# One scatter and one gather in turn, instead of four scatters and then four gathers

## The reference, cut to what matters

```python
row, col = edge_index[0], edge_index[1]                 # src, dst; the edges are sorted by dst
edge_input = concatenate([x[row], x[col], edge_attr])   # 128 + 128 + 16
h    = silu(edge_input @ eW1 + eb1)
m_ij = silu(h @ eW2 + eb2)
agg  = segment_sum(m_ij, row, num_segments=50000)
update = silu(concatenate([x, agg]) @ nW1 + nb1) @ nW2 + nb2
out  = layernorm(x + (x + update))
```

## Time and profile before

| | |
|---|---|
| median of the runs | 1695.71 us |
| the profiled execution, its own time | 1696.16 us |
| its span in the trace | 1694.7 us |
| granted TensorE clock over the span | 0.989 |
| PE busy | 1387.3 us, 82% |
| PE weight loads | 958.4 us, 57% |
| DVE busy | 939.6 us, 55% |
| ACT busy | 400.0 us, 24% |
| POOL busy | 1030.0 us, 61% |
| gathers L327, 392 | 384.3 us |
| scatters L370, 392 | 388.5 us |

### The profile page before, as it was taken

How to read it: one execution, slowest core, us unless ns; L and a number is a source line. 1 busy time by engine, 2 the same in 40 slices (tenths; PEclk the granted TensorE clock), 3 DMA queues, 4 the chain that set the end, 5 groups by cost and what they waited for, 6 DMA issues and landing times.

```text
span 1694.7 us, 25381 instructions
## 1 busy us (share of the span) xinstructions
PE 1387.3 (82%) x7834; PEld 958.4 (57%) x7834; DVE 939.6 (55%) x2971; ACT 400.0 (24%) x766; POOL 1030.0 (61%) x956
## 2 busy tenths in 40 slices
PE   1057888888888888888888888799997999999996
PEld 1054544444444444444444444455556999999996
DVE  6004555555555565555655556466763666666665
ACT  0001111111111111111111111121222555555555
POOL 7722666666666666666666666543444666666664
PEclk9999999999999999999999999899998999999998
DMA  9994343333433333333333333333326999999984
GB/s 376 412 365 115 89 112 101 105 105 100 112 100 106 106 100 110 102 106 106 100 110 102 103 108 100 89 97 102 96 94 222 305 297 301 305 299 302 304 297 161
DMA packets 156845, 284.99 MB, mean 168 GB/s; under 512 B 28046, under 2 KB 92322, under 8 KB 156708
## 3 DMA queue, kind: packets, MB, share of 16 engines
q1 hardware_dynamic: 110020, 162.78, 31.2%
q0 software_dynamic: 25088, 52.23, 10.8%
q10 hardware_dynamic: 21600, 68.32, 10.4%
HBM read 188.31 MB, written 94.91 MB: 167 GB/s over the span
## 4 chain that ended last, share of the span: by engine, by line
PE 60%; issue 14%; DVE 14%; another core or an unknown queue 11%; SPq 1%; DMA 0%; ACT 0%; POOL 0%; DVEq 0%; ACTq 0%
PE psum L544 10%; PE psum L534 8%; PE psum L489 7%; PE psum L486 7%; DVE junk L734 7%; PE psum L473 5%; PE psum L531 5%; PE psum L510 4%; PE psum L498 4%; DVE onehot L727 4%; PE psum L515 3%; PE psum L445 2%; DVE q L749 2%; PE psum L501 1%
## 5 line engine op out<-in xcount | busy, mean ns | idle before, releaser
L734 DVE CUSTOM_DVE_ANT_0 junk<-onehot,psum 128x625 f16<-128x625 f16 x392 | 316.4, 807 | 473.8 <-remote 232.9
L327 POOL DMA_INDIRECT x_src<-x_d,idx_src x392 | 384.3, 980 | 290.9 <-issue 129.4
L370 POOL DMA_INDIRECT table<-q,pos x392 | 388.5, 991 | 209.3 <-issue 113.7
L486 PE MATMUL psum<-onehot,after 128*128 128x512 f16 (+1 forms) x782 | 169.7, 298 | 178.8 <-issue 110.9
L486 PEld LDWEIGHTS psum<-onehot,after 128*128 128x128 f16 x782 | 51.8, 97 | 417.6 <-issue 416.8
L576 ACT ACTIVATE hT<-psum,b_e 128x512 f32<-128x512 f32 x98 | 67.4, 687 | 740.7 <-remote 617.0
L430 POOL TENSOR_TENSOR rstd<-var_eps,minus_half 128x5 f32<-128x5 f32 (+1 forms) x79 | 135.6, 1717 | 153.9 <-DVE var_eps L794 153.9
L473 PE MATMUL psum<-pick,window 128*128 128x128 f32 x1568 | 194.3, 278 | 7.2 <-DMA window<-x_d 7.2
L473 PEld LDWEIGHTS psum<-pick,window 128*128 128x128 f32 x1568 | 185.9, 195 | 7.6 <-DMA window<-x_d 7.6
L544 PE MATMUL psum<-w_out,uT 128*128 128x128 f32 (+1 forms) x782 | 188.5, 388 | 0.0
L544 PEld LDWEIGHTS psum<-w_out,uT 128*128 128x128 f32 (+1 forms) x782 | 178.9, 314 | 0.0
(11 more groups left out here) (85 smaller groups left out, 1533.5 us busy)
## 6 DMA issues: line engine op xcount, KB each, us to landing
window<-x_d SPq DMA_DIRECT2D x392, 128.0 KB
slots_in<-table SPq DMA_DIRECT2D x79, 528.0 KB, 5.0
table<-empty ACTq DMA_DIRECT2D x9, 4224.0 KB
x_in<-x_d SPq DMA_DIRECT2D x78, 320.0 KB, 4.2
xT_in<-xT_d SPq DMA_DIRECT2D x78, 320.0 KB, 3.8
out<-y_out ACTq DMA_DIRECT2D x78, 320.0 KB, 4.1
place<-place_dram SPq DMA_DIRECT2D x98, 128.0 KB
x_src<-x_d,idx_src POOLq DMA_INDIRECT x392
```

The costliest lines, as they stand in the source:

```text
L327: pool.indirect_dma_start(rows, None, x[:, :], bass.IndirectOffsetOnAxis(ap=idx[:, g * TILES + t:g * TILES + t + 1], axis=0)).then_inc(don ...
L370: pool.indirect_dma_start(table[:, :], bass.IndirectOffsetOnAxis(ap=pos[:, g * TILES + t:g * TILES + t + 1], axis=0), q[g % Q][:, t, :], None,
L486: nc.tensor.matmul(p_rank[:, cols], after[:], earlier[:, cols], start=False, stop=False, skip_group_check=True)
L734: V.tensor_tensor_reduce(out=junk[:], in0=onehot[g % 2][:, t, :], in1=p_rank, scale=1.0, scalar=0.0, op0=ALU.mult, op1=ALU.add, accum_out= ...
```

## The change

The function `scatter(g)` and the call of `gather_src(g + LEAD)` behind it become one function. It takes all waits first and then issues one scatter and one gather in turn, four times. Where there is no group left to gather (the last 22 of the 98 rounds) it only scatters.

```diff
-            def scatter(g):
+            def scatter_and_gather(g, ahead):
 
                 wait(pool, s_q, 2 * (g + 1))
                 wait(pool, s_pos, g + 1)
+                if ahead < GROUPS:
+                    wait(pool, s_src_turned, ahead - X_SRC + 1)
                 for t in range(TILES):
                     pool.indirect_dma_start(
                         table[:, :], bass.IndirectOffsetOnAxis(ap=pos[:, g * TILES + t:g * TILES + t + 1], axis=0),
                         q[g % Q][:, t, :], None,
                     ).then_inc(s_scattered[g % Q], 16)
+                    if ahead < GROUPS:
+                        gather(x_src[ahead % X_SRC][:, t * D:(t + 1) * D], idx_src, ahead, t, s_gathered[ahead % X_SRC])
...
                 for g in range(GROUPS):
-                    scatter(g)
-                    gather_src(g + LEAD)
+                    scatter_and_gather(g, g + LEAD)
```

## The result

The change makes the kernel slower: 1811.77 us (median of 4 runs, 1798.27 to 1822.51) against 1695.82 us on the same chip, a ratio of 1.067 [1.062, 1.071]. The profiled execution took 1813.31 us, 117.15 us more than the one before. The granted TensorE clock over the span fell from 0.989 to 0.928. The last group's first scatter starts 114.5 us later (at 1386.68 us, before at 1272.15), and what follows it takes 2.6 us more than before. So nearly the whole loss lies in the edge stage.

What follows compares the result with a forecast made beforehand. The prediction took a ring to bound the kernel: PE's posts wait for POOL's burst to end, the next burst for PE's post. 1696.16 - 37.5 - 2.1 + 5.2 = 1661.8 us, so 1661 us; eight-in-ten range 1590 to 1746.

Steps and rivals of the forecast that it cites:

- What bounds the kernel: Edge stage: PE's posts wait for the end of POOL's burst, the next burst for PE's post; 11.77 us a round.
- the late second four DMAs: Edge-stage rounds with eight DMAs: the second four cost 2.07 us a round, about 157 us over 76 rounds.
- the late h activation: ACT's L576 in the edge stage: starts 3.56 us after L503 ends, a sign that PE's posts arrive late.
- The instructions: POOL's bursts: same 392 gathers and 392 scatters, eight starts last 10.28 us before and after; cost 0.
- The added wait: Scatter(g) also waits until group g + 4 is turned, some 11.8 us later; ten q buffers cover it; cost 0.
- The first round and the last gathers: Ends of the edge stage: first burst four instead of eight, -2.07 us; last burst 20 DMAs instead of sixteen, +5.2 us.
- The order within the burst: Bursts of eight: fewer scatters late in the burst gain 0.50 us a round, 75 x -0.50 = -37.5 us.
- the price of the second burst: Early edge stage: 12.39 us from the second burst of eight to the next; as every round's length, 1746 us, the range's top.
- The count decides: Rival for the edge stage: DMA count, not kind, sets the round; it stays 11.77 us, total 1699 us; chance 0.24.
- The first rank post is caught too: Rival: PE's first rank post to DVE waits for the burst's end; 12.39 us a round, +46 us, 1745; chance 0.28.
- The posts pass freely: Rival: alternation removes the late posts, POOL bounds the edge stage at 10.28 us a round, 1587 us; chance 0.12.

Runs made afterwards that it cites:

- the changed kernel's second trace: The unaltered changed kernel run once more beside the kernel before, in a second comparison: 1747.03 us against 1716.26, ratio 1.018.
- the kernel with the later release: The changed kernel with one more wait at the head of each burst, for s_dst_turned of the same group: 1754.0 us, ratio 1.032.
- the kernel with the wait alone: The kernel before with the changed kernel's waits, but four scatters and then four gathers in blocks: 1702.54 us against 1702.49, ratio 1.000.
- the ladder: The kernel before with one to four gathers added, four rounds each, in rounds that otherwise only scatter: 1733.75 us (one run).
- three other orders of the same eight: Gather and scatter in turn with the kernel before's pairing (ratio 1.012), two of a kind in turn (1.017), and the changed kernel's strict alternation (1.067, again 1.018).

## Why the prediction was wrong

**What bounds the kernel** was read rightly in the main: a ring of a burst that holds posts and a post that releases the next burst. The condition without held posts fits its size: the edge stage is 175 us shorter there, and the late second four DMAs were priced at about 157 us. But the late h activation, the first sign that the prediction names, is not what closes the ring, since it is prompt in the trace of the slower kernel (0.04 us, median). Rounds of one length go with a late and with a prompt one: 12.39 us with 2.74 us in the changed kernel's second trace, 12.38 us with 0.04 us in the kernel with the later release (medians). And the matmuls of the preparation show that posts are not all that is held.

**The instructions.** Right: the burst lasts 10.05 us after the change, though the mean scatter grew by 21 ns (991 to 1012), about the 20 ns that the prediction allowed. The floor of 10.28 us a round is one of the ring only. Where posts pass, PE goes at 9.70 us a round (DVE's rank steps at 499.55 and 509.25 us) and POOL falls behind within its lead.

**The added wait.** Right at 0, shown by the kernel with the wait alone.

**The first round and the last gathers.** Right in kind. The start came out at -4.2 us instead of -2.07: a round of four DMAs took 10.31 us, and the two long rounds of 14.05 and 12.39 us that the kernel before begins with did not come again. The last burst had 20 DMAs, and the next came 37.27 us after it, 6.9 us more than before, where +5.2 was forecast.

**The order within the burst** is the step that failed. It took -0.50 us a round. The plain round became 0.47 us longer instead by the medians (0.47 in the second comparison as well, 12.39 against the 11.92 of blocks in the same comparison), and with the joined bursts the 75 rounds became 1.48 us longer on average. The argument was that fewer scatters late in the burst speak for a gain, as SP's long row and the late posts come only beside them. They do come together, but neither the scatters nor SP's loads are needed for the long round. SP's row fell from 7.15 us to 5.09 us as forecast, and nothing was gained. Without the window loads the rounds were 11.68 us. With gathers alone they were 13.77 us.

Its bounds, -1.49 to +2.28 us a round, did hold what happened: 110.8 us over 75 rounds are +1.48. But the range took only the price of the second burst as its upper end, and left out the cost of POOL going on without a pause, although showed it: a burst of sixteen with 30.34 us to the next. It was priced only for the last gathers.

**The count decides** was the nearest to the mechanism: the ladder shows five DMAs free and the sixth not, and the bytes don't matter in rounds of eight. But the count alone doesn't set the round. Blocks of four in either order give 11.77 and 11.79 us, while three other orders of the same eight give 11.95 to 12.39. That the round then stays at 11.77 us whatever the order did not follow. The rule of the Trainium skill, "SBUF — State Buffer", section "SBUF: two separate sides", on who waits for a port, was weighed there with the same result of 0. The plain round's +0.47 us is not 0. But what the traces show late are semaphore posts, of which that section doesn't speak. ACT's wait before L576 is one for a semaphore, so the prediction's remark that the trace does not bear the rule out went too far. No run here tests who waits for a port.

**The first rank post is caught too** had the right sign and the right round, 12.39 us, but the wrong post. The first rank step under the burst is read promptly after the change (end 815.14, DVE at 815.22). It is the next one, late already before by 2.67 us, that became 3.52 us late, and it is read no later after the burst's end than before; POOL's own restart is what moved. And its 1745 us left out the joined and nearly joined bursts, 86.6 us of the 114.5. In the second comparison, where these are absent, the loss of 31 us is near its +46.

**The posts pass freely** was set against the burst of sixteen, rightly: with alternation POOL did not pause in places, and that cost most.

**The clock** was no term. In the runs of sixteen PE is idle for up to 12 us and comes back at the lower level (L518 2.03 us against 1.11). That lies within the longer rounds of the table above, and what the clock alone costs there was not measured.

What stays open: why the order of the same eight DMAs moves the round between 11.8 and 12.4 us; whether POOL's issuing or its packets in flight hold the posts, and what slows PE's matmuls in the preparation; why the same program ran once without any held post; and what the change does in that condition, since the changed kernel was not run in it.

## What to carry to other kernels

When one engine's posts are late beside another engine's bursts, count how many DMA starts stand in a row, and find the longest row that costs nothing (here five) by adding starts one by one in a stretch with time to spare; then spread the starts so that fewer rounds exceed it. Here that, with the burst of sixteen near the end gone, gave 1.1% (0.989 [0.982, 0.995]). Be wary of reordering within a burst that releases itself: if the release can come before the burst ends, two bursts join. Here a run of sixteen cost 8.4 to 11.2 us, where the forecast gain was 0.50 us a round. And where a bound of the trace shows such a joined burst, its price belongs in the range.

## What the runs showed of the hardware

- Beside more than about five indirect DMAs of POOL in a row (0.94 to 1.2 us each, 0.30 us apart), semaphore posts of PE reach ACT, DVE and POOL late: about 3.5 us for eight, 12 us for sixteen. It happens with gathers alone, with scatters alone, with rows of a tenth the size (11.92 us a round, as the blocks of full rows in the ladder's kernel) and without SP's window loads; which post is late, and by how much, changes with these. Each of them was run once.
- In the preparation PE's own matmuls, which wait for nothing, come one in 2.80 us beside a row of 64 gathers and ten large fills, until 103.62 us, and in one row of 28.93 us for all 392 under the condition of 1490 us.
- In one comparison the same program took 1490.26 us, against 1696 to 1722 us in all others. The trace of another kernel of that comparison has neither the late posts nor the slow matmuls of the preparation: POOL issued for 840 us without a pause, and no rank step was read more than 0.5 us after its end from 200 to 1000 us. No run shows why.
- Whether bursts join varied for one and the same program. The traced execution of the changed kernel had five runs of sixteen in one comparison (ratio 1.067 [1.062, 1.071]) and, before the last gathers, none in another (1.018 [1.014, 1.022]).
